# Value projection and the transposes of the normalised outputs in one turn of the side bank

## Chip, cores and metric

The kernel runs on one core of a Trainium2 chip. The metric is the device time of one execution in microseconds, lower is better. Five engines work side by side, each through its own list in order: TensorE (PE in the profile), VectorE (DVE), ScalarE (ACT), GpSimd (POOL) and SyncE (SP), which issues DMAs. They wait for each other through semaphores.

## What is computed

32 items of 256 tokens by 128 features pass through two rounds of attention and expert network, each with a residual:

```python
x = x + attention_a(layernorm(x))     # 16 heads of 8, biases on q, k, v; two masked scores
x = x + experts(layernorm(x))         # top 2 of 8, gate from the mean over the tokens
x = x + attention_b(layernorm(x))     # 16 heads of 8, no bias
x = x + experts(layernorm(x))

# attention: softmax(q k^T * scale) v, then the output projection
# experts:   h = gelu(x Wd^T + bd) * weight; out = h Wu^T + weight * bu
```

## The kernel before

**Turns and steps.** Each item is worked on twice, once for each round: 64 turns (TURNS). Step n (from -6 to 70) has eight positions p = 0 to 7. In step n the stages of several turns are interleaved: the normalised input of turn n+5 is transposed, the queries and keys of n+4 and the values of n+3 are projected, the scores of n+2 are computed to find their maximum (`max_side`), the same scores of turn n are computed again with the maximum taken off, for the exponential (`exp_side`), the values of n are weighed (`weigh`, four groups g), and the outputs of n-1 are normalised and projected. Turn n-3 is normalised for the experts.

**Heads.** The 16 heads are eight pairs, one for each position: `max_side(n + 2, p)` writes the scores of one pair and VectorE reduces them (L598, `max_done`); `exp_side(n, p)` writes the transposed scores and ScalarE takes their exponential (L669, `exp_done`).

**The ring.** Both, and the two expert products `down` and `up`, write into `ring`, three PSUM pairs of two banks each. Which of the three a use gets is fixed by its place in the list `uses` (L288 to L298), filled position by position: scores, exps, then down where p == DOWN_AFTER and up where p == UP_AFTER, in the steps of BURSTS. `fill_pair` makes TensorE wait until the use three places before has been read: by VectorE (`max_done`, `added`) or by ScalarE (`exp_done`, `h_ready`). The places need not follow the order in which TensorE issues.

**The side bank.** `m_bank` is one PSUM bank for all small products: the transposes of the maximum (L886), the query and key projection (L898), the transposes of the unnormalised outputs (L910), the value projection (L920), the transposes of `o` (L931), those of `xy` (L943) and the output projection (L959). `fill_m` waits for the reader that the fill before has named, and names its own.

**Lists.** Each engine's order is written out by hand in its `step`: TensorE from L871, ScalarE from L660, VectorE from L581, GpSimd from L460, SyncE from L342. In a burst step (14 of them in steps 19 to 62, two more behind) four turns go through the experts: `down` (L815), four gelus on ScalarE (L722) with a change of its function table before and after, `up` (bias L830, product L838), and VectorE adds the result to x (L629). In step n of ScalarE, the copy of the values (L733) stands at p = 3, that of the transposed outputs `onT` (L739, L741) at p = 4, those of `xnT` and `normT` (L746, L749) at p = 5; each is preceded by that position's exponential.

Of the kernel before, what the change touches and what calls it, by code (L numbers as in the profile page):

```python
# [10 lines left out]
ACT = mybir.ActivationFunctionType  # L11
AX = mybir.AxisListType

P = 128
ITEMS, TOKENS, WIDTH = 32, 256, 128
# [40 lines left out]
def build(nc, x_dram_in, attn_w, attn_b, gate_w, down_w, down_b, up_w, up_b, tail_c, ident_c, iota_c, pick_c, out):  # L56
    ctx = ExitStack()
    with ctx:
# [31 lines left out]
        o = sb("o", [P, TILES, WIDTH])  # L90
        onT = sb("onT", [P, TOKENS])
# [62 lines left out]
        def fill_m(pe, reader, count):  # L154

            if m_reader[0] is not None:
                pe.wait_ge(*m_reader[0])
            m_reader[0] = (reader, count)
# [63 lines left out]
        BATCHES = ((0, 8), (8, 8), (16, 8), (24, 8), (32, 8), (40, 8), (48, 4), (52, 4), (56, 4), (60, 4))  # L222
        LATE, FIRST_BY_VECTOR = 56, 56
        BURSTS = (19, 23, 27, 31, 35, 39, 43, 47, 49, 51, 54, 56, 58, 62, 66, 70)
        DOWN_AFTER, UP_AFTER = 3, 4
        MIXING = 12
        WHICH, NBEST = 3, 4
        SPLITS = 5
# [15 lines left out]
        def group_at(n):  # L244

            return BURSTS.index(n) if n in BURSTS else None
# [10 lines left out]
        def live(turn):  # L257

            return 0 <= turn < TURNS
# [76 lines left out]
        with nc.Block() as block:  # L336
# [320 lines left out]
            def _(act):  # L657
                scalar_opening(act)

                def step(act, n, p):  # L660
# [49 lines left out]
                    if p == 3 and group_at(n) is not None:  # L710
# [11 lines left out]
                            nc.scalar.activation(hT[j][:, :], src, ACT.Gelu, bias=biasd[run][:, col:col + 1]).then_inc(h_ready, 1)  # L722
                        if n >= TURNS:
                            nc.scalar.activation(spare[:, len(BURSTS) + group:len(BURSTS) + group + 1], bqs[:, :], ACT.Exp)
                    if p == 3 and live(n + 3):

                        act.wait_ge(v_done, (n + 3) + 1)
                        act.wait_ge(set_up, VALUES_SET)
                        if live(n - 1):
                            act.wait_ge(pv_done, (n - 1) * GROUPS + GROUPS)  # L730
                        src = m_bank[:, 0:TOKENS].rearrange("p (b c d) -> p b c d", c=PER_GROUP, d=HEAD)
                        for g in range(IN_SHARE):
                            last = nc.scalar.copy(of_group((n + 3) % RING, g)[:, :, :, SUMS * g:SUMS * g + HEAD], src[:, g::IN_SHARE])  # L733
                        last.then_inc(v_ready, 1)
                    if p == 4 and live(n - 1):

                        act.wait_ge(oT2_done, (n - 1) + 1)
                        if n - 1 < ITEMS:
                            last = nc.scalar.activation(onT[:, :], m_bank[:, 0:TOKENS], ACT.Identity, bias=wa[:, 514:515])  # L739
                        else:  # L740
                            last = nc.scalar.copy(onT[:, :], m_bank[:, 0:TOKENS])  # L741
                        last.then_inc(onT_ready, 1)
                    if p == 5 and (live(n + 5) or live(n - 3)):
                        act.wait_ge(xyT_done, norm_steps(n))
                        if live(n + 5):
                            nc.scalar.copy(xnT[(n + 5) % 2][:, :], m_bank[:, 0:TOKENS]).then_inc(xnT_ready, 1)  # L746
                        if live(n - 3):
                            item = (n - 3) % ITEMS
                            nc.scalar.activation(normT[:, item:item + 1, :], m_bank[:, TOKENS:2 * TOKENS].unsqueeze(1), ACT.Copy,  # L749
                                                 accum_out=pooled[:, item:item + 1]).then_inc(yT_ready, 1)  # L750
# [10 lines left out]
            def _(pe):  # L761
# [32 lines left out]
                def exp_side(turn, p):  # L794

                    r = turn % RING
                    fill_pair(pe, "exps", turn, p)
                    if p == 0:
                        pe.wait_ge(max_in[turn % 2], turn // 2 * 32 + 32)
                    for k in range(TILES):  # L800
                        for a in range(2):
                            rows = slice(BLOCK * a, BLOCK * (a + 1))
                            last = nc.tensor.matmul(pair_of("exps", turn, p)[:, a, k * TOKENS:(k + 1) * TOKENS],  # L803
                                                    k_stack[r][rows, p, k * P:(k + 1) * P], q_stack[r][rows, p, :],
                                                    start=(k == 0), stop=(k == TILES - 1))
                    last.then_inc(t_done, 1)
# [12 lines left out]
                def up(group):  # L819

                    b = batch_of(group * GROUP)
                    fill_pair(pe, "up", group, 0)
                    pe.wait_ge(split_done, SPLITS * (b + 1))
                    pe.wait_ge(wu_ready, (group + 1) * GROUP)
                    for half in range(2):
                        bank = pair_of("up", group, 0)[:, half, :]
                        for j in range(2):
                            turn = group * GROUP + 2 * half + j
                            col = turn - BATCHES[b][0]
                            nc.tensor.matmul(bank[:, j * TOKENS:(j + 1) * TOKENS].rearrange("p (t d) -> p t d", t=TILES),  # L830
                                             pick[:, col:col + 1].broadcast_to([3 * ITEMS, P]),
                                             biasu_parts[b % 2][:, :].unsqueeze(1).broadcast_to([3 * ITEMS, TILES, WIDTH]),
                                             start=(j == 0), stop=False, skip_group_check=True)
                        for j in range(2):
                            pe.wait_ge(h_ready, group * GROUP + 2 * half + j + 1)
                            for t in range(TILES):
                                at = j * TOKENS + t * P
                                last = nc.tensor.matmul(bank[:, at:at + P], hT[2 * half + j][:, t * P:(t + 1) * P],  # L838
                                                        wu[(group * GROUP + 2 * half + j) % DEEP][:, :],
                                                        start=False, stop=(j == 1 and t == TILES - 1), skip_group_check=True)  # L840
                        last.then_inc(up_done, 1)
# [29 lines left out]
                def step(pe, n, p):  # L871
# [39 lines left out]
                        last.then_inc(on_done, 1)  # L911
                    if p == 3 and live(n):
                        weigh(n, 0)
                    if p == 4 and group_at(n) is not None:
                        down(group_at(n))
                    if p == 4 and live(n + 3):
                        wv = projections[(n + 3) // ITEMS][2]
                        fill_m(pe, v_ready, (n + 3) + 1)
                        for t in range(TILES):
                            last = nc.tensor.matmul(m_bank[:, t * P:(t + 1) * P], xnT[(n + 3) % 2][:, t * P:(t + 1) * P], wv,  # L920
                                                    start=(t == 0), stop=(t == TILES - 1), skip_group_check=True)
                        last.then_inc(v_done, 1)
                    if p == 5 and live(n):
                        exp_side(n, 4)
                    if p == 5 and group_at(n) is not None:
                        up(group_at(n))
                    if p == 5 and live(n - 1):
                        fill_m(pe, onT_ready, (n - 1) + 1)
                        pe.wait_ge(o_ready, (n - 1) + 1)
                        for t in range(TILES):  # L930
                            last = nc.tensor.transpose(m_bank[:, t * P:(t + 1) * P], o[:, t, :], ident[:, :])  # L931
                        last.then_inc(oT2_done, 1)
                    if p == 5 and live(n):
                        exp_side(n, 5)
                    if p == 5 and live(n):
                        weigh(n, 1)
                    if p == 6 and (live(n + 5) or live(n - 3)):
                        fill_m(pe, *((yT_ready, (n - 3) + 1) if live(n - 3) else (xnT_ready, (n + 5) + 1)))
                        pe.wait_ge(xy_ready, norm_steps(n))
                        for m in range(0 if live(n + 5) else 1, 2 if live(n - 3) else 1):  # L940
                            for t in range(TILES):
                                at = (m * TILES + t) * P
                                last = nc.tensor.transpose(m_bank[:, at:at + P], xy[(n + 5) % 2][:, m, t, :], ident[:, :])  # L943
                        last.then_inc(xyT_done, 1)
                    if p == 6 and live(n):
                        exp_side(n, 6)
                    if p == 7 and live(n):
                        weigh(n, 2)
                    if p == 7 and live(n):
                        exp_side(n, 7)  # L950
                    if p == PAIRS - 1 and batch_at(n, 0) is not None:
                        logits(batch_at(n, 0))
                    if p == PAIRS - 1 and live(n - 1):
# [58 lines left out]
```

## Time and profile before

| | |
|---|---|
| median of 3 runs | 989.06 us (989.05 to 990.65) |
| profiled execution | 990.56 us |
| its span in the profile | 987.4 us |
| TensorE busy | 917.8 us, 93% |
| VectorE busy | 787.2 us, 80% |
| ScalarE busy | 772.6 us, 78% |
| GpSimd busy | 666.2 us, 67% |
| mean granted TensorE clock | 0.982 |

The span is what the profiler sees between the first and the last instruction; about 3 us lie around it. In a timeline each row is a run of like instructions: start, length from first start to last end, engine, line, operation, tiles, shape and count, and in brackets how long the engine sat idle before it and what released it. Matmuls overlap each other, so the time that a block takes is read from one start to the next start, not from its length.

### The profile page before, as it was taken

What the parts mean: (1) busy time and instruction counts of PE and PEld (TensorE: products, weight loads), DVE (VectorE), ACT (ScalarE), POOL (GpSimd) and SP (SyncE); (2) the same over time, 40 slices, a digit from 0 to 9 for tenths busy, and PEclk for the clock granted to TensorE, in tenths of its full rate; (3) what the DMA queues carried; (4) which work ended last, traced back from release to release, by engine and by line L of the source; (5) the groups of instructions that cost most, each with busy time, mean ns of one, the idle gap of its engine ahead of it and who ended that gap; (6) DMA issues with size and microseconds to landing.
All of it is one profiled execution on the core that took longest, in us unless ns stands there. A gap on an engine that the chain in (4) does not pass through costs nothing.

```text
span 987.4 us, 27821 instructions
## 1 busy us (share of the span) xinstructions
PE 917.8 (93%) x10286; PEld 513.9 (52%) x10286; DVE 787.2 (80%) x1394; ACT 772.6 (78%) x1299; POOL 666.2 (67%) x1280
## 2 busy tenths in 40 slices
PE   2589999999999999999999999999999998999885
PEld 1345555545555555555655555555555555654544
DVE  1688888898888888888788887888788878778524
ACT  2168888888888888888888888888888877887863
POOL 8465666667775886768676786768687585764442
PEclk9899999999999999999999999999999999999987
DMA  6577555444444443444444343444444454344001
GB/s 183 150 219 204 154 149 168 141 152 142 135 140 121 150 134 120 145 121 146 119 138 149 121 143 119 153 119 128 136 136 142 125 153 123 118 137 135 5 22 43
DMA packets 144694, 131.66 MB, mean 133 GB/s; under 512 B 9616, under 2 KB 127536, under 8 KB 144432
## 3 DMA queue, kind: packets, MB, share of 16 engines
q1 hardware_dynamic: 143456, 128.49, 43.8%
q8 instruction: 82, 1.34, 0.6%
q10 hardware_dynamic: 1104, 1.41, 0.5%
q14 instruction: 52, 0.43, 0.1%
HBM read 73.76 MB, written 55.57 MB: 131 GB/s over the span
## 4 chain that ended last, share of the span: by engine, by line
PE 67%; ACT 10%; DVE 9%; POOL 5%; issue 4%; DMA 3%; SPq 1%; POOLq 1%; ACTq 1%; DVEq 0%
PE values_bank L774 21%; PE ring L789 11%; PE ring L803 10%; PE m_bank L898 6%; DVE nmax L598 5%; PE m_bank L910 4%; PE m_bank L959 3%; PE m_bank L943 3%; PE m_bank L920 3%; ACT probs L669 2%; PE m_bank L931 2%; ACT hT L722 2%; ACT L713 2%; DMA k_stack<-scratch 2%; DMA scratch<-parts 1%
## 5 line engine op out<-in xcount | busy, mean ns | idle before, releaser
L598 DVE TENSOR_REDUCE nmax<-ring 128x4 f32<-128x1024 f32 x512 | 605.1, 1219 | 98.0 <-PE ring L789 97.0
L669 ACT ACTIVATE probs<-ring 128x1024 f32<-128x1024 f32 x512 | 518.2, 1025 | 54.8 <-PE ring L803 50.4
L774 PE MATMUL values_bank<-probs,values 128*32 128x256 f32 x4096 | 274.9, 386 | 0.7 <-ACT probs L669 0.6
L789 PE MATMUL ring<-k_stack,q_stack 64*128 64x256 bf16 x2048 | 201.2, 277 | 22.7 <-DMA k_stack<-scratch 18.6
L489 POOL TENSOR_SCALAR xy<-x,mv,rstd 128x128 f32<-128x128 f32 x256 | 200.6, 793 | 7.9
L803 PE MATMUL ring<-q_stack,k_stack 64*128 64x256 bf16 x2048 | 189.4, 273 | 8.5 <-DVE nmax L598 7.2
L774 PEld LDWEIGHTS values_bank<-probs,values 128*32 128x32 f32 x4096 | 107.1, 109 | 89.8 <-issue 37.2
L413 POOL TENSOR_SCALAR mparts<-nmax 128x32 bf16<-128x32 f32 x64 | 13.9, 217 | 188.0 <-DVE nmax L598 187.8
L789 PEld LDWEIGHTS ring<-k_stack,q_stack 64*128 64x128 bf16 x2048 | 70.3, 95 | 132.0 <-issue 56.0
L803 PEld LDWEIGHTS ring<-q_stack,k_stack 64*128 64x128 bf16 x2048 | 78.0, 94 | 93.9 <-issue 52.0
L511 POOL TENSOR_TENSOR parts<-rest,parts 128x512 bf16<-128x512 f32 x64 | 74.1, 1158 | 5.4
L505 POOL TENSOR_TENSOR rest<-qk,parts 128x512 f32<-128x512 f32 x64 | 74.1, 1158 | 5.4
L482 POOL TENSOR_TENSOR rstd<-varp,minus_half 128x4 f32<-128x4 f32 (+1 forms) x72 | 69.4, 964 | 6.0
L529 DVE BATCH_NORM_STATS2 raw<-x 128x6 f32<-128x128 f32 x256 | 60.9, 280 | 10.8 <-DMA x<-in_x 10.7
L586 DVE TENSOR_TENSOR x<-x,m_bank 128x256 f32<-128x256 f32 x64 | 27.0, 421 | 49.9 <-PE m_bank L959 49.9
L733 ACT COPY values<-m_bank 128x128 f32<-128x128 f32 x128 | 29.1, 282 | 42.3 <-PE m_bank L920 42.3
L943 PE MATMUL m_bank<-ident,xy 128*128 128x128 f32 x256 | 44.9, 294 | 12.3 <-ACT wb L193 9.0
L696 ACT COPY oT<-values_bank 128x512 f32<-128x512 f32 x64 | 37.4, 585 | 20.1 <-PE values_bank L774 19.0
L502 POOL TENSOR_SCALAR parts<-qk 128x512 bf16<-128x512 f32 x64 | 39.5, 618 | 18.8 <-ACT qk L706 17.2
L746 ACT COPY xnT<-m_bank 128x256 f32<-128x256 f32 x64 | 23.8, 372 | 31.0 <-PE m_bank L943 30.8
L910 PE MATMUL m_bank<-ident,oT 128*128 128x128 f32 x256 | 41.9, 286 | 2.5 <-ACT oT L696 0.8
L508 POOL TENSOR_SCALAR parts<-rest 128x512 bf16<-128x512 f32 x64 | 39.5, 618 | 5.9
(102 smaller groups left out, 1084.0 us busy)
## 6 DMA issues: line engine op xcount, KB each, us to landing
q_stack<-scratch SPq DMA_DIRECT2D x128, 256.0 KB
k_stack<-scratch SPq DMA_DIRECT2D x128, 256.0 KB
scratch<-parts SPq DMA_DIRECT2D x128, 192.0 KB, 2.2
scratch<-parts SPq DMA_DIRECT2D x128, 128.0 KB, 2.2
scratch<-parts SPq DMA_DIRECT2D x128, 64.0 KB, 2.4
out<-x SPq DMA_DIRECT2D x16, 256.0 KB, 2.7
x<-in_x SPq DMA_DIRECT2D x3, 768.0 KB, 7.3
q_stack<-maxT SPq DMA_DIRECT2D x128, 12.0 KB
```

The costliest lines, as they stand in the source:

```text
L482: nc.gpsimd.tensor_tensor(rstd[i][:, both, :], varp[i][:, both, :], minus_half[:, both, :], ALU.pow).then_inc(rstd_done, 1)
L489: last = nc.gpsimd.tensor_scalar(xy[i][:, m, t, :], x[:, (turn % ITEMS) * TILES + t, :], mv[i][:, m, t, 0:1], rstd[i][:, m, t:t + 1], ALU. ...
L505: nc.gpsimd.tensor_tensor(rest[i][:, :, :], qk32[i][:, :, :], parts[i][:, 0], ALU.subtract).then_inc(rest_done, 1)
L511: nc.gpsimd.tensor_tensor(parts[i][:, 2], rest[i][:, :, :], parts[i][:, 1], ALU.subtract).then_inc(parts_ready, 1)
L529: last = nc.vector.bn_stats(raw[i][:, t, :], x[:, (turn % ITEMS) * TILES + t, :])
L598: nc.vector.tensor_reduce(dst, src, axis=AX.X, op=ALU.max, negate=True).then_inc(max_done, 1)
L669: nc.scalar.activation(probs[g % 2][:, c:c + 2, :, :], pair_of("exps", n, p)[:, :, :].rearrange("p x (k q) -> p x k q", k=TILES), ACT.Exp) ...
L774: last = nc.tensor.matmul(values_bank[32 * c:32 * (c + 1), a * TOKENS:(a + 1) * TOKENS], values[turn % RING][:, k, PER_GROUP * g + c, :], ...
L789: last = nc.tensor.matmul(pair_of("scores", turn, p)[:, a, t * TOKENS:(t + 1) * TOKENS], q_stack[z][rows, p, t * P:(t + 1) * P], k_stack[z ...
L803: last = nc.tensor.matmul(pair_of("exps", turn, p)[:, a, k * TOKENS:(k + 1) * TOKENS], k_stack[r][rows, p, k * P:(k + 1) * P], q_stack[r][ ...
L910: last = nc.tensor.transpose(m_bank[:, at:at + P], oT[(n - 1) % 2][:, a, t * P:(t + 1) * P], ident[:, :])
L943: last = nc.tensor.transpose(m_bank[:, at:at + P], xy[(n + 5) % 2][:, m, t, :], ident[:, :])
```

## The change

The value projection (turn n+3) and the transposes of `o` (turn n-1) had a fill of `m_bank` each, at p = 4 and between the two exp-side pairs of p = 5. Now they share one, behind the exp-side pairs 4 and 5, in the two halves of the bank: the projection in columns 0 to 255, the transposes in 256 to 511. On TensorE `down` moves ahead of the score pair of p = 4, `up` behind exp-side pair 5 (and UP_AFTER goes from 4 to 5, which changes the places in the ring), exp-side pair 6 ahead of the transposes of `xy`, exp-side pair 7 ahead of the third weighing. On ScalarE the copy of `onT` and then that of the values stand at p = 5, and those of `xnT` and `normT` at p = 6.

```diff
-        DOWN_AFTER, UP_AFTER = 3, 4
+        DOWN_AFTER, UP_AFTER = 3, 5
@@ ScalarE
-                    if p == 3 and live(n + 3):
+                    if p == 5 and live(n - 1):
+
+                        act.wait_ge(oT2_done, (n - 1) + 1)
+                        if n - 1 < ITEMS:
+                            last = nc.scalar.activation(onT[:, :], m_bank[:, TOKENS:2 * TOKENS], ACT.Identity, bias=wa[:, 514:515])
+                        else:
+                            last = nc.scalar.copy(onT[:, :], m_bank[:, TOKENS:2 * TOKENS])
+                        last.then_inc(onT_ready, 1)
+                    if p == 5 and live(n + 3):
 
                         act.wait_ge(v_done, (n + 3) + 1)
+                        if live(n - 1):
+                            act.wait_ge(oT2_done, (n - 1) + 1)
                         act.wait_ge(set_up, VALUES_SET)
...
-                    if p == 4 and live(n - 1):
-
-                        act.wait_ge(oT2_done, (n - 1) + 1)
-                        if n - 1 < ITEMS:
-                            last = nc.scalar.activation(onT[:, :], m_bank[:, 0:TOKENS], ACT.Identity, bias=wa[:, 514:515])
-                        else:
-                            last = nc.scalar.copy(onT[:, :], m_bank[:, 0:TOKENS])
-                        last.then_inc(onT_ready, 1)
-                    if p == 5 and (live(n + 5) or live(n - 3)):
+                    if p == 6 and (live(n + 5) or live(n - 3)):
                         act.wait_ge(xyT_done, norm_steps(n))
@@ TensorE
-                    if p == 4 and group_at(n) is not None:
+                    if p == 3 and group_at(n) is not None:
                         down(group_at(n))
-                    if p == 4 and live(n + 3):
+                    if p == 5 and live(n):
+                        exp_side(n, 4)
+                        exp_side(n, 5)
+                    if p == 5 and group_at(n) is not None:
+                        up(group_at(n))
+                    if p == 5 and (live(n + 3) or live(n - 1)):
+                        fill_m(pe, *((v_ready, (n + 3) + 1) if live(n + 3) else (onT_ready, (n - 1) + 1)))
+                    if p == 5 and live(n + 3):
                         wv = projections[(n + 3) // ITEMS][2]
-                        fill_m(pe, v_ready, (n + 3) + 1)
                         for t in range(TILES):
...
-                    if p == 5 and live(n):
-                        exp_side(n, 4)
-                    if p == 5 and group_at(n) is not None:
-                        up(group_at(n))
                     if p == 5 and live(n - 1):
-                        fill_m(pe, onT_ready, (n - 1) + 1)
                         pe.wait_ge(o_ready, (n - 1) + 1)
                         for t in range(TILES):
-                            last = nc.tensor.transpose(m_bank[:, t * P:(t + 1) * P], o[:, t, :], ident[:, :])
+                            last = nc.tensor.transpose(m_bank[:, TOKENS + t * P:TOKENS + (t + 1) * P], o[:, t, :], ident[:, :])
                         last.then_inc(oT2_done, 1)
                     if p == 5 and live(n):
-                        exp_side(n, 5)
-                    if p == 5 and live(n):
                         weigh(n, 1)
+                    if p == 6 and live(n):
+                        exp_side(n, 6)
...
-                    if p == 6 and live(n):
-                        exp_side(n, 6)
+                    if p == 7 and live(n):
+                        exp_side(n, 7)
                     if p == 7 and live(n):
                         weigh(n, 2)
-                    if p == 7 and live(n):
-                        exp_side(n, 7)
```

## Rows read from the trace of the kernel before

**Rows 1.** The page: busy shares, and two groups (busy us, mean ns | idle before).
```profile
PE 917.8 (93%) x10286; PEld 513.9 (52%) x10286; DVE 787.2 (80%) x1394; ACT 772.6 (78%) x1299; POOL 666.2 (67%) x1280
...
L598 DVE TENSOR_REDUCE nmax<-ring 128x4 f32<-128x1024 f32 x512 | 605.1, 1219 | 98.0 <-PE ring L789 97.0
L669 ACT ACTIVATE probs<-ring 128x1024 f32<-128x1024 f32 x512 | 518.2, 1025 | 54.8 <-PE ring L803 50.4
```

**Rows 2.** Timeline of TensorE in an ordinary step: start us, length us, instructions.
```profile
452.97 0.39 PE L789 MATMUL ring<-k_stack,q_stack 64*128 64x256 bf16 x4
453.29 0.71 PE L920 MATMUL m_bank<-wb,xnT 128*128 128x128 f32 x4
453.94 0.39 PE L789 MATMUL ring<-k_stack,q_stack 64*128 64x256 bf16 x4
...
454.55 0.44 PE L931 MATMUL m_bank<-ident,o 128*128 128x128 f32 x2
454.91 0.39 PE L803 MATMUL ring<-q_stack,k_stack 64*128 64x256 bf16 x4
455.24 1.07 PE L774 MATMUL values_bank<-probs,values 128*32 128x256 f32 x16
456.24 0.39 PE L789 MATMUL ring<-k_stack,q_stack 64*128 64x256 bf16 x4
...
457.69 1.07 PE L774 MATMUL values_bank<-probs,values 128*32 128x256 f32 x16
...
459.02 0.71 PE L959 MATMUL m_bank<-wa,onT 128*128 128x128 f32 x4
459.66 0.39 PE L789 MATMUL ring<-k_stack,q_stack 64*128 64x256 bf16 x4
459.89 0.38 PE L803 MATMUL ring<-q_stack,k_stack 64*128 64x256 bf16 x4
460.21 0.39 PE L789 MATMUL ring<-k_stack,q_stack 64*128 64x256 bf16 x4
```

**Rows 3.** Timeline of TensorE in step 61, which has no value projection.
```profile
920.26 0.75 PE L789 MATMUL ring<-k_stack,q_stack 64*128 64x256 bf16 x8
...
921.98 0.39 PE L803 MATMUL ring<-q_stack,k_stack 64*128 64x256 bf16 x4 [0.38 <-DVE nmax L598]
```

**Rows 4.** Timeline of TensorE in a burst step.
```profile
478.64 0.39 PE L789 MATMUL ring<-k_stack,q_stack 64*128 64x256 bf16 x4
...
480.79 0.61 PE L920 MATMUL m_bank<-wb,xnT 128*128 128x128 f32 x4
481.33 0.39 PE L789 MATMUL ring<-k_stack,q_stack 64*128 64x256 bf16 x4
...
481.96 0.39 PE L830 MATMUL ring<-biasu_parts,pick 96*128 96x256 bf16 x2
...
484.20 0.38 PE L931 MATMUL m_bank<-ident,o 128*128 128x128 f32 x2
...
484.96 1.07 PE L774 MATMUL values_bank<-probs,values 128*32 128x256 f32 x16
```

**Rows 5.** Timeline of ScalarE in the same burst step.
```profile
480.36 1.55 ACT L722 ACTIVATE hT<-ring,biasd 128x256 f32<-128x256 f32 x4
...
482.27 1.28 ACT L669 ACT_TABLE_LOAD   x1
```

**Rows 6.** Timeline of TensorE around two waits for the maximum's parts.
```profile
804.14 0.27 PE L886 MATMUL m_bank<-identb,mparts 128*128 128x128 bf16 x2 [1.46 <-POOL mparts L419]
...
808.53 0.39 PE L789 MATMUL ring<-k_stack,q_stack 64*128 64x256 bf16 x4
...
870.27 0.27 PE L886 MATMUL m_bank<-identb,mparts 128*128 128x128 bf16 x2 [1.37 <-POOL mparts L419]
...
873.18 0.39 PE L789 MATMUL ring<-k_stack,q_stack 64*128 64x256 bf16 x4
```

**Rows 7.** Windows: stretch, its length, busy us of each engine, granted clock, DMA.
```profile
804.40:806.00 1.60, 1.60 (x17) 0.57 (x16) 0.19 (x1) 0.36 (x1) 1.49 (x2) 0.50 0.39 87
```

## The prediction

> **What bounds the kernel now.** I read the page's busy shares first, then TensorE's timeline of one ordinary step and of one burst step, then the rows in which TensorE waited. TensorE is busy 93% of the span; VectorE and ScalarE, each with a long instruction per pair (a 1.22 us reduction, a 1.03 us exponential), 80% and 78% [rows 1]. In an ordinary step TensorE's instructions follow each other without a gap [rows 2]: the step lasts as long as TensorE's list plus the waits that its in-order queue meets. So the question is what the new order of that list does to its waits, and these come from the ring: three PSUM pairs, so that every use waits for the reader of the use three places before.
>
> Below, sN and eN are the score pair and the exp-side pair of position N; w0 to w3 are the four weighings (L774); V is the value projection (L920), oT2 the transposes of `o` (L931), xyT those of `xy` (L943), wo the output projection (L959).
>
> Order before, from w0 on: s4, [down], V, s5, e4, [up], oT2, e5, w1, s6, xyT, e6, s7, w2, e7, wo. Order after: [down], s4, s5, e4, e5, [up], V, oT2, w1, s6, e6, xyT, s7, e7, w2, wo. ("down" and "up" in 14 burst steps only.)
>
> **Ring places.** Places are dealt by the list `uses`, not by the order of issue: sN has place 2N, eN has 2N+1 in an ordinary step. So e5 (11) waits for the reduction of s4 (8), and e7 (15) for that of s6 (12), before and after. What changes is how much stands between them.
>
> **Ordinary step, s4 to w1.** Before: s4 at 452.97, w1 at 455.24, 2.27 us; e5 comes 1.94 us after s4 and doesn't wait, since V, s5, e4 and oT2 lie between [rows 2]. After, only s5 and e4 do, 0.23 us each (s0 to e0 [rows 2]), and e5 must wait. The price of that wait stands in this trace: in the step in which no value projection is due any more, s4 starts at 920.26 and e5 at 921.98, after a wait for the reduction of L598 [rows 3]. That is 1.72 us, made of the pair (0.4) and the reduction (1.22 [rows 1]). Behind e5 come e5 itself, 0.33 (454.91 to 455.24), V, 0.65 (453.29 to 453.94), and oT2, 0.36 (454.55 to 454.91), less 0.10 for the second of two blocks of the same shape: V behind "down" takes 0.54 (480.79 to 481.33 [rows 4]) and not 0.65. Sum 1.72 + 0.33 + 0.65 + 0.26 = 2.96 us, so **+0.69**. V and oT2 covered the reduction of s4; moved behind e5, they stand bare.
>
> **Ordinary step, w1 to the next s0.** Before: 455.24 to 459.66, 4.42 us [rows 2]. After: w1 to s6 1.00; s6 to e7 again at least 1.72, as e7 now stands ahead of w2 and only e6, xyT and s7 lie between, whose own time is 1.36 or so with s6 (before, w2's 1.0 lay there too); e7 0.33; w2 1.0; wo 0.64 (459.02 to 459.66). Sum 4.70: **+0.28**. One thing is gained: s1 came 0.32 after e0 instead of 0.23 [rows 2], held by the exponential of e7, which now is a microsecond earlier: **-0.10**. An ordinary step: **+0.87 us**.
>
> The moved copies on ScalarE (onT, then values, then behind e6 xnT and normT) lie in time that it has idle; V's copy no longer holds up exponential 4, but that exponential wasn't waited for. xyT must wait for V's copy: 0.4 us to spare by the same sums. A wait of ScalarE for oT2 holds exponential 6 behind it, which needs w1 anyway. VectorE, GpSimd and SyncE keep their lists; SyncE's waits on e7 are met earlier. The turn of the side bank that is saved costs nothing now: no wait on it shows between s4 and w1 [rows 2]. Cost of these edits: 0, between -0.1 and +0.2 a step.
>
> **Burst step.** With UP_AFTER = 5 the places are down 8, s4 9, e4 10, s5 11, e5 12, up 13. So s5 now waits for all four gelus of "down" (before it waited for s4's reduction and ran at 481.33), and "up" waits for exponential 4 (before, for the gelus, which were done by then). Take the step of rows 4 and 5. Down and s4 start at 478.64, but the gelus are tied to ScalarE's table load, not to "down": last one done at 480.36 + 1.55 = 481.91. s5 at 481.95, e4 at 482.18, done 482.57. Now ScalarE must load the exponential's table, 1.28 us, and run it, 1.02 [rows 1, 5]: done 484.92, up at 484.98. Before, ScalarE's chain ran while TensorE did "up"; now "up" waits for it. Then up 2.24 (481.96 to 484.20), V 0.54, oT2 0.26: w1 at 488.02 against 484.96 [rows 4]: **+3.06**. With the second half (+0.28) and s1 (-0.10): **+3.24 us**.
>
> Where the table load stands is a choice: the trace has it after e4's end and after the copies, which fits both orders. I take it behind the wait for e4; if it could start right after the gelus, exponential 4 ends 0.7 us earlier, +2.5 instead of +3.2. The Trainium skill (ScalarE: Activation LUTs, What happens when an `exp` ACTIVATE runs) says that the compiler places the load right before the ACTIVATE, which speaks for the later order; its figure for a switch with its drain, about 2.66 us against the 1.28 that the trace shows as busy, would add an estimated 1.4 us a burst if a drain were bare here, and no row shows one.
>
> **The clock.** In a burst step TensorE now sits idle about 1.0 us before s5 and 2.0 before "up", within four microseconds. The trace shows a case: after a wait of 1.46 us [rows 6] the granted clock was 0.50, the 1.2 GHz level, in the next 1.6 us [rows 7], and from the maximum's transposes to s3 the step took 4.39 us (804.14 to 808.53), against 2.91 (870.27 to 873.18) after a wait of 1.37 that left the clock up [rows 6]. Price 1.48 us. I take it for each burst; bounds 0 and 2.5 (a second dip). The ordinary step's idle time of 0.9 is below both, so no dip there.
>
> **Sum.** Score pairs are issued in steps 0 to 61. 49 ordinary x 0.87 = 42.6; less 1.6 for two steps in which TensorE waited for GpSimd's parts of the maximum [rows 6], which absorb it; 13 bursts x 3.24 = 42.1; 13 x 1.48 = 19.2. Steps 62 to 70 and the opening: 0 (ScalarE and DMA bound). Together +102.3. The profiled execution took 990.56 us (span 987.4), so 1092.9; it is 1.5 us above the median of 989.06. Forecast: **1091.5 us**.
>
> **Rivals.**
> 1. *The clock stays up in bursts.* For it: a wait of 1.37 us left it up. Against: idle time here is more than twice that. -19.2: 1072.
> 2. *The table load goes ahead of the wait* (clock as forecast). -0.7 x 13 = -9: 1082.
> 3. *The clock falls in ordinary steps too.* 0.9 us of idle time each 13.7; against it the row that stayed up with 1.37. +49 x 1.48 = +73: 1164; some of them only, 1115 to 1164.
> 4. *Fewer changes of tile shape pay, and the ring doesn't bind* (the faster side). A run of pairs costs 0.23 for each pair that another follows and 0.32 or 0.33 for the last (s0 against s4 [rows 2]). The new order has 6 runs instead of 9 a step: 3 x 0.10 x 62 = 18.6 us, 971. It decides if s4's reduction is done within 0.7 us of s4's start; the reduction alone takes 1.22 [rows 1], and rows 3 show the wait. The Trainium skill (TensorEngine Tiling (Array Packing), Key Properties) says the same in general, that changing the tiling mode drains TensorE; by this rule alone the change is a gain, and the trace agrees with the rule (0.10 a change), but not that it is the larger term.
> 5. *Only part of the waits is bare*, since the longer step frees the other engines earlier than I worked out, or bursts hide more: 1000 to 1060.
>
> **How the numbers follow.** Forecast case 0.56, rival 1 0.15, rival 2 0.11, rival 3 0.06, rival 4 0.04, rival 5 0.06, no change 0.02. The range takes in the forecast with its bounds (clock at 2.5 a burst: +13; small terms +-10) and rivals 1 and 2: 1060 to 1112. Faster by over 0.2% 0.04, within 0.2% (about what a measurement of this kernel can tell from no change) 0.02, slower 0.94.
>
> **What would show it.** Right: e5 in every ordinary step starts with a wait of about 1 us for L598, 1.72 after s4; e7 with a short one 1.72 after s6; ordinary steps last 13.7 us; s5 of a burst waits for L722, "up" for L669, with 2 us of idle time, and the granted clock is 0.5 behind it. Wrong: e5 without a wait; the sum fails most easily in the burst steps, through the clock and the table load.

## The result

| | before | after |
|---|---|---|
| median | 989.86 us (4 runs, 989.05 to 992.27) | 1091.88 us (4 runs, 1091.51 to 1092.57) |
| ratio | | 1.103, 95% interval 1.101 to 1.105 |
| profiled span | 987.4 us | 1089.7 us |
| TensorE busy | 917.8 us, 93% | 926.9 us, 85% |
| mean granted TensorE clock | 0.982 | 0.960 |

The change makes the kernel 10% slower. The same number of instructions (27821) runs in 102 us more, and only 9 us of it is busy time of TensorE. The page of the changed kernel, against [rows 1]: busy shares, granted clock by fortieths of the span in tenths, and two of the groups whose waits grew (busy us, mean ns | idle before, its releaser):

```profile
PE 926.9 (85%) x10286; PEld 536.4 (49%) x10286; DVE 788.0 (72%) x1394; ACT 764.6 (70%) x1299; POOL 666.7 (61%) x1280
...
PEclk9899999999999999999998989999989998989996
...
L669 ACT ACTIVATE probs<-ring 128x1024 f32<-128x1024 f32 x512 | 516.7, 1025 | 181.6 <-PE ring L805 176.6
...
L805 PE MATMUL ring<-q_stack,k_stack 64*128 64x256 bf16 x2048 | 186.0, 272 | 61.7 <-DVE nmax L598 61.3
```

The exp-side pairs (L803 before, L805 after) now wait 61.3 us for the reductions, 7.2 before. TensorE's list of waits after (total us, times, longest) names the three kinds that were forecast; no other grew by more than 0.7 us:

```profile
PE ring L805 <- DVE nmax L598: 61.3, 119, 2.0
PE ring L832 <- ACT probs L669: 29.1, 13, 2.2
...
PE ring L791 <- ACT hT L722: 13.5, 13, 1.1
```

**An ordinary step after.** TensorE's timeline from s4 to the next s1, to set beside [rows 2]. The first row holds s4 and s5:

```profile
486.65 0.75 PE L791 MATMUL ring<-k_stack,q_stack 64*128 64x256 bf16 x8
487.24 0.38 PE L805 MATMUL ring<-q_stack,k_stack 64*128 64x256 bf16 x4
488.37 0.39 PE L805 MATMUL ring<-q_stack,k_stack 64*128 64x256 bf16 x4 [0.75 <-DVE nmax L598]
488.69 0.71 PE L928 MATMUL m_bank<-wb,xnT 128*128 128x128 f32 x4
489.24 0.38 PE L934 MATMUL m_bank<-ident,o 128*128 128x128 f32 x2
489.55 1.07 PE L776 MATMUL values_bank<-probs,values 128*32 128x256 f32 x16
490.55 0.39 PE L791 MATMUL ring<-k_stack,q_stack 64*128 64x256 bf16 x4
...
492.27 0.39 PE L805 MATMUL ring<-q_stack,k_stack 64*128 64x256 bf16 x4 [0.20 <-DVE nmax L598]
492.59 1.07 PE L776 MATMUL values_bank<-probs,values 128*32 128x256 f32 x16
...
494.24 0.39 PE L791 MATMUL ring<-k_stack,q_stack 64*128 64x256 bf16 x4
```

The names sN, eN, w0 to w3, V, oT2, xyT and wo are those of the prediction. s4 to e5 is 1.72 us and s6 to e7 is 1.72 us, to the hundredth what the wait of [rows 3] gave. s4 to w1 is 2.90 us (before 2.27), w1 to s0 4.69 (before 4.42).

**A burst step after**, to set beside [rows 4] and [rows 5]; first TensorE, then ScalarE's table load, then windows (stretch, length, busy us of TensorE, its weight loads, VectorE, ScalarE and GpSimd with their instructions, granted clock, DMA):

```profile
513.88 1.99 PE L817 MATMUL ring<-normT,wd 128*128 128x256 f32 x8
515.81 0.39 PE L791 MATMUL ring<-k_stack,q_stack 64*128 64x256 bf16 x4
517.22 0.39 PE L791 MATMUL ring<-k_stack,q_stack 64*128 64x256 bf16 x4 [1.01 <-ACT hT L722]
517.45 0.60 PE L805 MATMUL ring<-q_stack,k_stack 64*128 64x256 bf16 x8
520.29 0.39 PE L832 MATMUL ring<-biasu_parts,pick 96*128 96x256 bf16 x2 [2.24 <-ACT probs L669]
...
523.92 0.85 PE L928 MATMUL m_bank<-wb,xnT 128*128 128x128 f32 x4
524.60 0.38 PE L934 MATMUL m_bank<-ident,o 128*128 128x128 f32 x2
524.91 1.07 PE L776 MATMUL values_bank<-probs,values 128*32 128x256 f32 x16
```
```profile
517.91 1.28 ACT L669 ACT_TABLE_LOAD   x1 [0.75 <-PE ring L805]
519.21 1.94 ACT L669 ACTIVATE probs<-ring 128x1024 f32<-128x1024 f32 x2
```
```profile
518.10:520.20 2.10, 0.00 (x0) 0.00 (x0) 1.17 (x3) 2.09 (x3) 0.23 (x1) 1.00 0.75 224
...
521.00:522.00 1.00, 1.00 (x8) 0.88 (x7) 0.00 (x0) 0.15 (x1) 0.00 (x0) 0.50 0.00 0
522.00:523.00 1.00, 1.00 (x6) 1.00 (x5) 0.69 (x1) 0.00 (x0) 0.00 (x0) 0.50 0.00 0
```

ScalarE is idle 0.75 us before the table load and is released by e4: the load does stand behind that wait. TensorE then idles 2.24 us, and the granted clock falls from 1.00 to 0.50 about 0.7 us after it has begun to work again (at 520.29). "Up" takes 3.63 us in place of 2.24.

**Account.** From the start of the maximum's transposes (L886 before, L888 after, once a step) to the next, step by step and summed against the trace before: the 13 burst steps lost 65.1 us (forecast 42.1 + 19.2 = 61.3), all others 37.4 (forecast 42.6 - 1.6 = 41.0). With -0.1 ahead of and behind these steps that makes the 102.3 by which the span grew. The forecast was 3.8 us too low for the bursts and 3.6 too high for the rest: the two errors cancel, and that the total matches this closely is luck.

### The profile page after: what moved, and what is told of

The parts are those of the page before. It is cut to its first block, busy times and chain, and to the rows that moved or that the text cites. A ratio compares the mean times of both kernels' runs of the same rounds, so it can differ in the third digit from the quotient of the medians.

```text
span 1089.7 us, 27821 instructions
## 1 busy us (share of the span) xinstructions
PE 926.9 (85%) x10286; PEld 536.4 (49%) x10286; DVE 788.0 (72%) x1394; ACT 764.6 (70%) x1299; POOL 666.7 (61%) x1280
## 4 chain that ended last, share of the span: by engine, by line
PE 61%; DVE 18%; ACT 10%; POOL 3%; issue 3%; DMA 2%; ACTq 1%; POOLq 0%; SPq 0%; DVEq 0%
PE values_bank L776 20%; DVE nmax L598 15%; PE ring L791 8%; PE ring L805 8%; PE m_bank L900 5%; PE ring L840 4%; PE m_bank L960 4%; PE m_bank L912 3%; PE m_bank L928 3%; ACT probs L669 2%; ACT hT L722 2%; ACT L669 2%; DMA k_stack<-scratch 1%; PE ring L832 1%; ACT qk L705 1%
## 5 line engine op out<-in xcount | busy, mean ns | idle before, releaser
L598 DVE TENSOR_REDUCE nmax<-ring 128x4 f32<-128x1024 f32 x512 | 605.2, 1220 | 127.1 <-PE ring L791 126.3
L805 PE MATMUL ring<-q_stack,k_stack 64*128 64x256 bf16 x2048 | 186.0, 272 | 61.7 <-DVE nmax L598 61.3
L791 PE MATMUL ring<-k_stack,q_stack 64*128 64x256 bf16 x2048 | 196.7, 276 | 36.8 <-DMA k_stack<-scratch 17.7
L805 PEld LDWEIGHTS ring<-q_stack,k_stack 64*128 64x128 bf16 x2048 | 83.8, 94 | 132.2 <-DVE nmax L598 112.9
L629 DVE TENSOR_TENSOR x<-x,ring 128x512 f32<-128x512 f32 x32 | 22.0, 688 | 67.1 <-PE ring L840 67.1
L840 PE MATMUL ring<-wu,hT 128*128 128x128 f32 x256 | 51.2, 367 | 0.0
L840 PEld LDWEIGHTS ring<-wu,hT 128*128 128x128 f32 x256 | 48.4, 281 | 1.4
```

The source lines that it names most:

```text
L598: nc.vector.tensor_reduce(dst, src, axis=AX.X, op=ALU.max, negate=True).then_inc(max_done, 1)
L791: last = nc.tensor.matmul(pair_of("scores", turn, p)[:, a, t * TOKENS:(t + 1) * TOKENS], q_stack[z][rows, p, t * P:(t + 1) * P], k_stack[z ...
```

## The experiments

Each is timed beside the kernel before, whose median was 990.31 us beside experiments 1, 3, 6 and 7, and 989.18 beside 2, 4, 5 and 8; ratios are to these. Differences from the changed kernel go by its 1091.88 us, taken on another occasion, on which the kernel before had 989.86. Step lengths and granted clocks are read from the trace of each run, steps as in the account. A dip is a stretch in which the granted clock is 0.50.

### 1. The burst edits undone

```diff
-        DOWN_AFTER, UP_AFTER = 3, 5
+        DOWN_AFTER, UP_AFTER = 3, 4
-                    if p == 3 and group_at(n) is not None:
+                    if p == 4 and group_at(n) is not None:
                         down(group_at(n))
...
                     if p == 5 and live(n):
                         exp_side(n, 4)
-                        exp_side(n, 5)
                     if p == 5 and group_at(n) is not None:
                         up(group_at(n))
+                    if p == 5 and live(n):
+                        exp_side(n, 5)
```

> The changed kernel with its burst edits undone: UP_AFTER 4 again, down behind the score pair of p = 4, up between exp-side pairs 4 and 5. What is left of the change is the shared turn behind e5 and the new places of e6 and e7. Theory (two separate losses: bare reduction waits in every step, bare gelu and exponential waits with a clock dip in bursts): ordinary steps stay at 13.76 and 13.62 us, bursts fall from 21.7 to about 17.7 us; 1036 us in all, 49 x 0.79 + 13 x 0.77 above the kernel before. Rival (the loss of the bursts comes from the late turn of the side bank and the copies behind it, not from the places of down and up): bursts stay at 20 us and more, 1065 us or more.

Measured 1031.73 us, 1.043 of before (1.039 to 1.046). Ordinary steps 13.76 and 13.62 as in the changed kernel; the bursts without a batch of the gate 17.6 us. Against the trace before, the 13 bursts lost 6.4 us and the others 37.6. So nine tenths of the bursts' 65 us go when "down" and "up" get their places back, and the ordinary loss is wholly that of the shared turn's place with e6 and e7. No burst has a dip here.

### 2. The burst edits alone

```diff
-        DOWN_AFTER, UP_AFTER = 3, 4
+        DOWN_AFTER, UP_AFTER = 3, 5
-                    if p == 4 and group_at(n) is not None:
+                    if p == 3 and group_at(n) is not None:
                         down(group_at(n))
...
                     if p == 5 and live(n):
                         exp_side(n, 4)
-                    if p == 5 and group_at(n) is not None:
-                        up(group_at(n))
...
                     if p == 5 and live(n):
                         exp_side(n, 5)
+                    if p == 5 and group_at(n) is not None:
+                        up(group_at(n))
```

> The kernel before with the burst edits alone: UP_AFTER 5, down ahead of the score pair of p = 4, up behind exp-side pair 5; the turns of the side bank as before. Theory: ordinary steps stay at 12.97 and 12.84; in bursts up waits for exponential 4 for 1.8 us, +2.3 us each and 1020 us in all, or 1040 if the clock falls. Rival (the burst edits hurt only together with the late turn of the bank): bursts within 0.7 us of before, 1000 us or less.

Measured 1037.34 us, 1.049 (1.046 to 1.052). Ordinary steps stay at 12.97 and 12.84. The bursts lost 46.2 us, the others 2.2. The two waits are shorter than in the changed kernel, as V stands ahead of the first and oT2 ahead of the second:

```profile
494.80 0.39 PE L789 MATMUL ring<-k_stack,q_stack 64*128 64x256 bf16 x4
495.13 0.71 PE L920 MATMUL m_bank<-wb,xnT 128*128 128x128 f32 x4
496.21 0.39 PE L789 MATMUL ring<-k_stack,q_stack 64*128 64x256 bf16 x4 [0.37 <-ACT hT L722]
...
499.28 0.39 PE L830 MATMUL ring<-biasu_parts,pick 96*128 96x256 bf16 x2 [1.77 <-ACT probs L669]
```

In 8 of the 13 bursts the clock fell, in the wait ahead of "up" or within 1 us behind its start; these lost 3.8 to 4.7 us. Of the five without a dip of their own, the last with pairs lost 2.40, two that also hold a batch of the gate 3.08 each, and one, into which a dip of the step ahead reaches, 3.05; step 54 lost 0.91, against a step of the kernel before that had a dip of its own [rows 6, 7]. The rival (burst edits harmless by themselves) falls. But the burst edits alone cost the bursts 46.2 us and the rest of the change alone 6.4 (experiment 1), against 65.1 with both: some 12 us arise only when they meet, since V and oT2 then stand behind both waits, which are 1.0 and 2.24 us in place of 0.37 and 1.77, with 12 dips in place of 8.

### 3. The shared turn ahead of e5

```diff
-                        exp_side(n, 5)
-                    if p == 5 and group_at(n) is not None:
-                        up(group_at(n))
                     if p == 5 and (live(n + 3) or live(n - 1)):
                         fill_m(pe, *((v_ready, (n + 3) + 1) if live(n + 3) else (onT_ready, (n - 1) + 1)))
...
                         last.then_inc(oT2_done, 1)
+                    if p == 5 and live(n):
+                        exp_side(n, 5)
+                    if p == 5 and group_at(n) is not None:
+                        up(group_at(n))
@@ ScalarE, the copies of onT and of the values
-                    if p == 5 and live(n - 1):
+                    if p == 4 and live(n - 1):
...
-                    if p == 5 and live(n + 3):
+                    if p == 4 and live(n + 3):
```

> The changed kernel with its shared turn put ahead of e5: s4, s5, e4, V, oT2, e5, [up], w1 (ScalarE's two copies at p = 4 behind exponential 4). The turn is still one, the copies are still two in a row. Theory (V and oT2 covered the reduction of s4): s4 to w1 falls from 2.90 to 2.05 us, ordinary steps to 12.9 and 12.8; bursts also fall by 0.85; 1039 us, or 1020 if the idle time in front of up becomes so short that the clock stays up. Rival (sharing one turn is itself what costs, since the copies of both must be done before the transposes of xy): ordinary steps stay above 13.4 us, 1080 us or more.

Measured 1028.05 us, 1.038 (1.035 to 1.042). TensorE in an ordinary step, s4 and s5 in the first row:

```profile
449.63 0.75 PE L791 MATMUL ring<-k_stack,q_stack 64*128 64x256 bf16 x8
...
450.53 0.71 PE L925 MATMUL m_bank<-wa,xnT 128*128 128x128 f32 x4
451.08 0.38 PE L931 MATMUL m_bank<-ident,o 128*128 128x128 f32 x2
451.39 0.39 PE L805 MATMUL ring<-q_stack,k_stack 64*128 64x256 bf16 x4
451.71 1.07 PE L776 MATMUL values_bank<-probs,values 128*32 128x256 f32 x16
```

s4 to e5 is 1.76 us without a wait, s4 to w1 2.08 (theory 2.05), and the ordinary steps take 12.90 and 12.80 us. One shared turn costs nothing; its place behind e5 costs 0.8 us. The bursts also dropped, by 28.3 us together or 2.2 each. The clock stayed up in all of them, with waits of about 1.0 and 1.27 us; by experiment 6 that is 22.9 of the 28.3. The order is the rest, 5.4 us: 0.67 in most bursts and nothing in the five that also hold a batch of the gate, where the gain comes back as a longer wait of e7 (0.75 in the changed kernel):

```profile
441.34 0.39 PE L805 MATMUL ring<-q_stack,k_stack 64*128 64x256 bf16 x4 [1.42 <-DVE nmax L598]
```

### 4. Half of one reduction

```diff
+                        if p == 4:
+                            src = src[:, :, :, 0:TOKENS // 2]
                         nc.vector.tensor_reduce(dst, src, axis=AX.X, op=ALU.max, negate=True).then_inc(max_done, 1)
```

> The changed kernel with the reduction of position 4 alone over half of the keys (the maximum that it takes off is then that of half the keys, for this pair of heads): 512 elements a partition in place of 1024. Nothing on TensorE is touched. Theory (e5 waits for just this reduction): the wait falls by the half of 1.22 us less a fixed part, some 0.53 us, in each of the 49 ordinary steps, none in bursts, where e5 waits for nothing: ordinary steps 13.2 and 13.1, 1066 us. Rival (e5 is held by the bank or by ScalarE, and VectorE is only the last that the profile can name): no change of the steps, 1092 us.

Measured 1069.71 us, 1.082 (1.079 to 1.086). Ordinary steps 13.22 and 13.09, 0.54 less, and the wait of e5 has shrunk from 0.75 to 0.22 (s4 again in the first row; the edit adds two lines, L600 is L598):

```profile
475.44 0.75 PE L793 MATMUL ring<-k_stack,q_stack 64*128 64x256 bf16 x8
...
476.62 0.39 PE L807 MATMUL ring<-q_stack,k_stack 64*128 64x256 bf16 x4 [0.22 <-DVE nmax L600]
```

Nothing on TensorE, ScalarE or in the side bank was touched. This shows that the reduction of s4 and not another reader holds e5. The bursts hardly changed (they lost 66.7 us, with a dip in all 13), as forecast.

### 5. e7 back behind the third weighing

```diff
-                    if p == 7 and live(n):
-                        exp_side(n, 7)
                     if p == 7 and live(n):
                         weigh(n, 2)
+                    if p == 7 and live(n):
+                        exp_side(n, 7)
```

> The changed kernel with one edit undone: e7 stands behind the third weighing again. Theory (e7 waits 0.2 to 0.3 us for the reduction of s6, and s1 gets 0.1 us back): 0.16 us less in each of 62 steps, 10 us, 1082 us; ordinary steps 13.6 and 13.46. Rival (the wait only moves, since the reduction of s7 or exponential 7 is then late for the next step): steps within 0.05 us of now, 1090 us.

Measured 1075.98 us, 1.086 (1.082 to 1.089). Ordinary steps 13.61 and 13.47, 0.15 less, where 0.16 was worked out; the wait didn't move elsewhere. That makes 8.1 us over the steps without a burst. The total fell by more than the 10 us forecast, since the bursts lost 59.2 us instead of 65.1. Of these 5.8 us some 2.0 are the same 0.15 in 13 bursts. Another 1.9 come from the five bursts with a batch of the gate, in which e7 waited 0.75 us for its reduction (0.19 in the others) and now doesn't wait. The rest is the clock, which stayed up in two bursts instead of one.

### 6. Idle work in the bursts

```diff
+                    if p == 4 and group_at(n) is not None and live(n + 2):
+                        if p == 4:
+                            fill_m(pe, o_ready, (n - 1) + 1)
+                        for _ in range(2):
+                            nc.tensor.matmul(m_bank[:, 0:TOKENS], ident[:, :], xnT[(n + 3) % 2][:, :], start=True, stop=True)
                     if p == 5 and live(n):
                         exp_side(n, 4)
                         exp_side(n, 5)
+                    if p == 5 and group_at(n) is not None and live(n + 2):
+                        if p == 4:
+                            fill_m(pe, o_ready, (n - 1) + 1)
+                        for _ in range(4):
+                            nc.tensor.matmul(m_bank[:, 0:TOKENS], ident[:, :], xnT[(n + 3) % 2][:, :], start=True, stop=True)
                     if p == 5 and group_at(n) is not None:
                         up(group_at(n))
```

> The changed kernel with idle work for TensorE in the 13 burst steps that have score pairs: two matmuls of 256 columns ahead of s5 and four ahead of up, written to the side bank, which the value projection overwrites; their result is used by nothing. Theory (the clock falls to half because TensorE stood idle): granted clock 1.0 behind up, up back from 3.6 to 2.2 us and V from 0.68 to 0.55, bursts 1.5 us shorter each, 1073 us. Rival (up is slow there for another reason, such as its operands arriving late, and the low clock is a detail): bursts as long as now or longer by what the extra matmuls take, 1092 us or more.

Measured 1070.84 us, 1.081 (1.078 to 1.084): 78 matmuls more (six in each of 13 bursts), and 21 us less than the changed kernel. TensorE in a burst, then a window over "up":

```profile
516.87 1.99 PE L930 MATMUL m_bank<-xnT,ident 128*128 128x256 f32 x8
519.18 0.39 PE L832 MATMUL ring<-biasu_parts,pick 96*128 96x256 bf16 x2 [0.32 <-ACT probs L669]
...
521.42 0.61 PE L938 MATMUL m_bank<-wb,xnT 128*128 128x128 f32 x4
```
```profile
519.00:521.00 2.00, 1.82 (x17) 1.78 (x18) 0.49 (x1) 1.04 (x2) 0.00 (x0) 1.00 0.13 38
```

"Up" takes 2.24 us again at a granted clock of 1.00. The bursts lost 42.2 us, where the sum without the clock had said 42.1. No burst has a dip. The difference from 65.1, 22.9 us, is the clock's share in the bursts: 12 dips of 1.4 to 2.9 us, while the burst that had none in the changed kernel (step 27) takes the same 21.78 us in both. The steps without a burst still lost 39.5.

### 7. The exponential's table loaded right behind the gelus

```diff
-                        if n >= TURNS:
+                        if True:
                             nc.scalar.activation(spare[:, len(BURSTS) + group:len(BURSTS) + group + 1], bqs[:, :], ACT.Exp)
```

> The changed kernel with one exponential of a single column directly behind the four gelus, so that the table of the exponential is loaded before ScalarE waits for e4. Theory (the load stands behind the wait for e4 and lies bare in front of exponential 4): exponential 4 starts 0.6 us earlier, up too, 13 x 0.6 = 8 us less, 1084 us. Rival (the load is hidden, or what up waits for is not that exponential): no change, 1092 us.

Measured 1065.98 us, 1.078 (1.073 to 1.082): 26 us less, where 8 were forecast. The wait of "up" is 1.60 us instead of 2.24, 0.64 less where 0.6 was worked out. What was missed is the clock: with 1.60 us of idle time it stayed up in 11 of the 13 bursts. Two bursts of this execution; the first had the shorter wait ahead of s5 (0.90 against 1.01) and dipped, the second did not. Another one that dipped (step 49) had the same 1.01 and 1.60 as the second:

```profile
390.81 0.39 PE L832 MATMUL ring<-biasu_parts,pick 96*128 96x256 bf16 x2 [1.60 <-ACT probs L669]
391.04 1.63 PE L840 MATMUL ring<-wu,hT 128*128 128x128 f32 x8
...
515.81 0.39 PE L832 MATMUL ring<-biasu_parts,pick 96*128 96x256 bf16 x2 [1.60 <-ACT probs L669]
516.03 1.06 PE L840 MATMUL ring<-wu,hT 128*128 128x128 f32 x8
```

### 8. A version that covers the reductions

From the changed kernel: the turn as in experiment 3 between e4 and e5, in bursts right behind "down"; the bursts as in experiment 1; e7 as in experiment 5; the table as in experiment 7. What remains of the change is one shared turn and e6 ahead of xyT. The main part of the edit:

```diff
+                    at = 4 if group_at(n) is not None else 5
                     if p == 5 and live(n):
                         exp_side(n, 4)
-                        exp_side(n, 5)
                     if p == 5 and group_at(n) is not None:
                         up(group_at(n))
-                    if p == 5 and (live(n + 3) or live(n - 1)):
+                    if p == at and (live(n + 3) or live(n - 1)):
                         fill_m(pe, *((v_ready, (n + 3) + 1) if live(n + 3) else (onT_ready, (n - 1) + 1)))
...
+                    if p == 5 and live(n):
+                        exp_side(n, 5)
```

> A version of its own: the shared turn stands between e4 and e5 (in bursts behind down), with its copies behind exponential 4; e7 is back behind the third weighing; the burst edits are undone; one exponential of a column behind the gelus loads its table early. e6 stays ahead of the transposes of xy. Theory (fewer changes of tile shape pay as soon as the reductions are covered): ordinary steps 12.75 and 12.62, bursts 0.2 us less than before, 977 us against 990. Rival (the ring, at 1.72 us from s4 to e5, takes all of it back): within 3 us of the kernel before.

Measured 981.27 us, 0.992 of before (0.990 to 0.994): 0.8% faster than the kernel before, and 10% faster than the changed one. An ordinary step:

```profile
448.12 0.75 PE L791 MATMUL ring<-k_stack,q_stack 64*128 64x256 bf16 x8
...
449.88 0.39 PE L805 MATMUL ring<-q_stack,k_stack 64*128 64x256 bf16 x4
450.20 1.07 PE L776 MATMUL values_bank<-probs,values 128*32 128x256 f32 x16
```

s4 to e5 is 1.76 us and doesn't wait, s4 to w1 2.08 against 2.27. Ordinary steps take 12.75 and 12.65 us (forecast 12.75 and 12.62), bursts without a batch of the gate mostly 0.22 less than before, bursts with one nothing. The total is 4 us above the forecast. The steps without a burst gained 6.1 us rather than some 10: the first two, in the opening, took 2.2 us more than before (the stretch ahead of them 1.5 less), and several steps around the gate's batches gained nothing. The bursts gained 1.9.

## Why the prediction came out as it did

- **Ring places and the wait of e5: right.** 1.72 us from s4, from one row of a single step [rows 3]. Experiments 3 and 4 show it from two sides, cover and reduction.
- **The rest of s4 to w1: 0.06 us too long.** V to oT2 took 0.55 and oT2 to w1 0.31; I had 0.65 and 0.26. The saving of 0.10 belongs to V, which is followed by its own shape, and oT2 saved half as much (0.31 for 0.36). An ordinary step lost 0.79 instead of 0.87, the mis-sized term being +0.69, which measured +0.63, and a rounding in +0.28, which measured +0.27. The 0.10 at s1 came: s1 starts 0.22 to 0.23 after e0, and 0.32 again in experiment 8, where e7 is back behind w2.
- **The burst's order: right.** s5 waits for the gelus, "up" for exponential 4, the table load stands behind e4. The Trainium skill (ScalarE: Activation LUTs, Step-by-step: what each stage is for) puts the load right before the ACTIVATE, and this trace agrees: the row at 517.91. The Trainium skill's figure for a switch with its drain, about 2.66 us (ScalarE: Activation LUTs, What ACT_TABLE_LOAD costs), is not borne out here: the exponential starts 1.30 us after the load starts. Without the clock a burst lost 3.24 us by my sum; in experiment 6 most lost 3.22, and the 13 together 42.2 for 42.1 forecast.
- **Within that a term was left out:** the five bursts that also hold a batch of the gate lost 3.6 us in experiment 6, the others 3.2. VectorE's small operations for the batch now stand behind the later "up", in front of the reduction that e7 waits for: that wait is 0.75 us in these bursts and 0.19 in the others, and with e7 put back (experiment 5) a batch burst without a dip lost 3.1 like the others. That 42.1 meets 42.2 is luck: 5 x 0.4 = 2 us are hidden by the burst of step 54, which lost only 1.7 in experiment 6, since the kernel before had a dip of its own there [rows 6, 7] and the changed kernel has none at its start.
- **The clock: right in kind, too small.** I priced a dip at 1.48 in each of 13 bursts, 19.2 us; the bursts lost 22.9 by it, in 12 dips of 1.9 on average, the four longest 2.1 to 2.9. The burst without one (step 27) had 2.24 us in front of "up" and 1.15 ahead of s5, and so had that of step 19, which dipped.
- **Rival 1** (no dips) is what experiment 6 made: 1070.84 against 1072 given. **Rival 2** (table ahead of the wait) is experiment 7; its 1082 missed that the shorter wait also spares dips. **Rival 3** came true in one of the 49 steps, step 55, which I had not seen: there eight small operations of VectorE for a batch stand ahead of the reduction of s6, e7 waits 1.98 us, and the clock falls 0.5 us after its start:

```profile
923.28 0.39 PE L805 MATMUL ring<-q_stack,k_stack 64*128 64x256 bf16 x4 [1.98 <-DVE nmax L598]
923.60 1.83 PE L776 MATMUL values_bank<-probs,values 128*32 128x256 f32 x16
```

That step lost 1.97 us; with e7 behind w2 (experiment 5) it waits 1.17, keeps its clock and loses 0.04. In the kernel before it waited 1.76 and kept its clock too. **Rival 4** had its condition right: whether the reduction of s4 is covered decides. Experiment 8 covers it, and fewer changes of tile shape then pay: the pairs of an ordinary step form eight runs instead of nine, and V stands beside oT2, two changes less, for 0.22 and 0.19 us a step. That it is the changes that pay fits the 0.10 of each and is not shown by a run of its own. The ring kept the six runs of the changed kernel from paying. **Rival 5** did not occur: the waits came as bare as forecast.
- **The arithmetic** has slips that don't matter: 1092.9 less 1.5 is 1091.4, the upper end with both bounds would be 1115, and pair and reduction make 1.62 of the 1.72 us, which was read from the row.

## What to carry to other kernels

In a rotation of a few buffers, count for each use what stands on the issuing queue between it and the use whose reader it waits for: that work is cover, even when it looks as if it only interrupted a run of like instructions. Look in the trace for the one step in which the cover is missing by chance, as in [rows 3]; it has the price of the wait ready to read. Where an edit opens an idle stretch on TensorE, add the clock to its cost: here the waits of 1.0 and 2.24 us in the bursts cost 22.9 of the 102 us through the clock, and an edit that shortened the second by 0.64 us gave most of that back.

## What the runs showed of the hardware

Waits of TensorE ahead of s5 and ahead of "up", and in how many of the 13 bursts the granted clock fell to 0.50, run by run:

| run | waits, us | bursts with a dip |
|---|---|---|
| changed kernel, experiments 4 and 5 | 0.9 to 1.15, 2.24 | 12, 13 and 11 |
| experiment 2 | 0.26 to 0.65, 1.77 | 8 |
| experiment 7 | 0.9 to 1.14, 1.60 | 2 |
| experiment 3 | 0.9 to 1.14, 1.27 | none |
| experiment 6 | none, 0.32 | none |

Equal waits in one execution gave both outcomes; what decides between them stays open. The same holds for longer waits elsewhere: 1.46 us [rows 6] and 1.98 (step 55) had a dip, 1.37 [rows 6] and 1.76 (step 55 before) had none. Six matmuls with no use for their result, put into the idle time of each burst, made the kernel 2% faster (1070.84 us against 1091.88).
